# A value bias moved from the values of x to the copy of the message in a graph attention kernel

## The reference

```
q_base = elu(q_encoding @ w_qin.T + b_qin)
for t in range(4):
    cmd = q_base @ w_qt[t].T + b_qt[t]
    xc = x_ctx * mask
    x_joint = [x_loc, xc, pl(x_loc) * pc(xc)]
    q = lin(x_joint, w_q, b_q)
    k = lin(x_joint, w_k, b_k) * lin(cmd, w_pk, b_pk)
    v = lin(x_joint, w_v, b_v) * lin(cmd, w_pv, b_pv)
    e = edge scores of q and k by edge type, leaky relu, absent edges at -9e15
    prob = softmax(e)
    message = prob @ v
    x_ctx = lin([xc, message], w_mu, b_mu)
y = lin([x_loc, x_ctx], w_cb, b_cb)
```

## Time and profile before

| | us |
|---|---|
| median of 3 runs | 588.87 |
| lowest and highest | 586.61, 593.03 |
| span of the profiled execution | 569.6 |
| median less span | 19.3 |
| TensorE busy in the span | 513.9 (90%) |
| VectorE busy | 431.6 (76%) |
| ScalarE busy | 399.8 (70%) |
| GpSimd busy | 286.4 (50%) |

### The profile page before, as it was taken

How to read it: one execution, slowest core, us unless ns; L and a number is a source line. 1 busy time by engine, 2 the same in 40 slices (tenths; PEclk the granted TensorE clock), 3 DMA queues, 4 the chain that set the end, 5 groups by cost and what they waited for, 6 DMA issues and landing times. The chain is left out here.

```text
span 569.6 us, 14419 instructions
## 1 busy us (share of the span) xinstructions
PE 513.9 (90%) x4673; PEld 342.2 (60%) x4673; DVE 431.6 (76%) x1156; ACT 399.8 (70%) x1150; POOL 286.4 (50%) x511
## 2 busy tenths in 40 slices
PE   5997699999999999999889999898999788789991
PEld 3665466666666666665345565555655445568880
DVE  3589878888888888886545577868777878897882
ACT  4557578888888888887557687666777656558991
POOL 0587742222222222110144365858687757377884
PEclk9998999999999999999989999999999989869996
DMA  8600999999999300000100000011114003425530
GB/s 346 279 2 7 280 264 271 255 268 256 270 261 267 95 0 0 1 2 0 38 0 2 2 2 2 30 31 39 38 49 169 29 30 96 123 95 137 136 86 11
DMA packets 48535, 60.77 MB, mean 107 GB/s; under 512 B 2488, under 2 KB 45509, under 8 KB 47574
## 3 DMA queue, kind: packets, MB, share of 16 engines
q1 hardware_dynamic: 45686, 53.59, 35.4%
q0 software_dynamic: 2784, 6.37, 3.2%
HBM read 18.30 MB, written 42.10 MB: 106 GB/s over the span
## 5 line engine op out<-in xcount | busy, mean ns | idle before, releaser
L1565 DVE TENSOR_REDUCE nm<-SC 128x8 f32<-128x1024 f32 x64 | 75.3, 1219 | 33.6 <-PE SC L1076 33.0
L1465 DVE TENSOR_REDUCE room_w<-SC 128x512 f32<-128x2048 f32 x32 | 73.3, 2290 | 13.8 <-PE SC L927 13.8
L2079 ACT ACTIVATE room_p<-ST 128x512 f32<-128x512 f32 (+1 forms) x96 | 64.1, 740 | 25.6 <-PE ST L1094 25.6
L600 POOL TENSOR_TENSOR spread<-parts,units 128x48 bf16<-128x48 bf16 x32 | 8.8, 275 | 119.8 <-DVE parts L1455 119.8
L1985 ACT ACTIVATE room_w<-room_w,shift 128x128 f32<-128x128 f32 x128 | 49.7, 390 | 20.4 <-DVE shift L1472 20.4
L1976 ACT ACTIVATE room_w<-ST,cv 128x128 f32<-128x128 f32 x128 | 36.5, 367 | 17.0 <-PE ST L942 17.0
L1113 PE MATMUL SC<-room_p,room_w 128*32 128x128 f32 x1024 | 35.3, 279 | 9.2 <-DVE nm L1565 7.7
L798 POOL DMA_INDIRECT out<-room_v,id_r x39 | 38.7, 993 | 9.4 <-issue 7.0
L942 PEld LDWEIGHTS ST<-room_w 128*128 128x128 f32 x256 | 33.0, 191 | 15.2 <-issue 13.0
L1994 ACT ACTIVATE room_w<-room_w,inv 128x128 f32<-128x128 f32 x128 | 41.0, 409 | 0.8 <-DVE inv L1477 0.8
L636 POOL TENSOR_TENSOR ctx_t<-room_w 128x512 f32<-128x512 f32 x24 | 30.5, 1270 | 21.9 <-PE SC L927 20.6
(11 more groups left out here) (297 smaller groups left out, 1398.4 us busy)
## 6 DMA issues: line engine op xcount, KB each, us to landing
sorted_rows<-w SPq DMA_DIRECT2D x8, 4290.0 KB, 43.7
room_v<-sorted_rows SPq DMA_DIRECT2D x39, 130.0 KB, 2.1
x_t<-xT SPq DMA_DIRECT2D x2, 1024.0 KB, 8.1
ctx_t<-adj SPq DMA_DIRECT2D x1, 2048.0 KB, 16.5
room_w<-x SPq DMA_DIRECT2D x8, 256.0 KB, 2.9
room_w<-mask SPq DMA_DIRECT2D x1, 1536.0 KB
w<-weights SPq DMA_DIRECT2D x1, 1228.0 KB, 8.6
x_t<-w SPq DMA_DIRECT2D x1, 1032.0 KB, 5.0
```

What stands on the lines that cost most here:

```text
L1465: dve.tensor_reduce(logit[:, :, :], SC[:, :, :].rearrange("p b (i m) -> p b m i", i=TYPES), AX_X, ALU.max)\
L1565: dve.tensor_reduce(nm[:, v % 2, 2 * PER_R * pair:2 * PER_R * (pair + 1)], SC[:, 2 * pair:2 * pair + 2, :].rearrange("p r (i n) -> p (r i) ...
L2079: act.activation(ex[:, v % 2, first:last, :], ST[:, first:last, :], ACT.Exp)\
```

## The change

GpSimd no longer adds b_v to `vx`, and VectorE no longer waits for it. Instead b_v is one of the bias columns. GpSimd makes once `cvb` = `cv` * b_v (a column for each round and batch). `message_out` adds it: the Copy with a scale column becomes Identity with a scale column and a bias column. b_v leaves the row vectors, and the wait for them moves behind the rounds.

```diff
@@ setup, GpSimd
+            pool.wait_ge(cmd_ready, CV_OUT)
+            pool.tensor_scalar(cvb[:, :, :].rearrange("p t b -> p (t b)"), cv[:, :, :].rearrange("p t b -> p (t b)"),
+                               bias("bv"), None, ALU.mult).then_inc(S("cvb_ready"), 1)
             pool.wait_ge(S("u_out"), 1)
@@ GpSimd
-            def add_bias(g):
-
-                pool.wait_ge(vx_even, g + 1)
-                pool.wait_ge(vx_odd, g + 1)
-                bs = slice(g * GB, (g + 1) * GB)
-                pool.tensor_tensor(vx[:, bs, :], vx[:, bs, :], R("bv").unsqueeze(1).broadcast_to([128, GB, D]), ALU.add)\
-                    .then_inc(S("vx_ready"), 1)
...
             pool.wait_ge(S("first_ready"), 1)
             first_products(0)
-            pool.wait_ge(in_bv, 16)
-            add_bias(0)
             first_context(1)
...
             first_locals(1)
-            add_bias(1)
...
-                if opens(s) and opens(s + 5):
-                    add_bias(s + 5)
...
+            pool.wait_ge(in_bv, 16)
             pool.wait_ge(S("va_zero"), 2)
@@ VectorE
             columns(0, 0, 0)
-            dve.wait_ge(S("vx_ready"), 1)
             v_out(0, 0)
...
-                    if opens(s + 4):
-                        dve.wait_ge(S("vx_ready"), s + 5)
                     v_out(s + 4, n)
@@ ScalarE
             def message_out(s, t, g):
                 act.wait_ge(msg_done, s + 1)
+                if isinstance(s, int) and s == 0:
+                    act.wait_ge(S("cvb_ready"), 1)
                 for b in range(GB):
                     scale = cv[:, bass.ds(t, 1), g * GB + b:g * GB + b + 1].rearrange("p t b -> p (t b)")
-                    op = act.activation(msg_s[:, b * N:(b + 1) * N], M[:, b, :], ACT.Copy, scale=scale)
+                    shift_v = cvb[:, bass.ds(t, 1), g * GB + b:g * GB + b + 1].rearrange("p t b -> p (t b)")
+                    op = act.activation(msg_s[:, b * N:(b + 1) * N], M[:, b, :], ACT.Identity, scale=scale, bias=shift_v)
                 op.then_inc(msg_evac, 1)
```

More of the change, by code:

```diff
@@ L45 @@
 BIAS = {n: i for i, n in enumerate(("qin", "pl", "pc", "q", "k", "mu", "cb", "pk", "pv", "qt0", "qt1", "qt2",
-                                    "qt3", "init", "iq", "ik", "ln1g", "ln1b", "bo"))}
+                                    "qt3", "init", "iq", "ik", "ln1g", "ln1b", "bo", "bv"))}
 NW_FIRST = WCOLS["wk"][0]
 RCOLS = {"iv": (0, 128), "bo": (128, 256), "bog": (256, 268), "ln1g": (268, 396), "ln1b": (396, 524),
-         "ln2g": (524, 652), "ln2b": (652, 780), "gate": (780, 792), "bv": (792, 920)}
-NR = 920
+         "ln2g": (524, 652), "ln2b": (652, 780), "gate": (780, 792)}
+NR = 792
 HEADS = 16
@@ L196, in build @@
         cv = sb("cv", [128, T_ITER, B])
+        cvb = sb("cvb", [128, T_ITER, B])
         bq_w1 = sb("bq_w1", [128, TYPES])
@@ L617, in _ @@
             place(1)
-            add_bias(2)
             pool.wait_ge(v_done, 2)
@@ L622, in _ @@
             place(2)
-            add_bias(3)
             bias_parts()
@@ L628, in _ @@
             first_products(4)
-            add_bias(4)
             pool.memset(pad_row, 0.0).then_inc(S("spread_ready"), 1)
@@ L1494, in _ @@
             columns(1, 0, 1)
-            dve.wait_ge(S("vx_ready"), 2)
             v_out(1, 1)
@@ L1500, in _ @@
             columns(2, 0, 2)
-            dve.wait_ge(S("vx_ready"), 3)
             v_out(2, 2)
@@ L1506, in _ @@
             columns(3, 0, 3)
-            dve.wait_ge(S("vx_ready"), 4)
             v_out(3, 3)
@@ L2222, in layouts @@
                  ("iq", f["in_proj_b"][:D]), ("ik", f["in_proj_b"][D:2 * D]), ("bo", f["out_proj_b"]), ("ln1g", f["ln1_g"]),
-                 ("ln1b", f["ln1_b"])):
+                 ("ln1b", f["ln1_b"]), ("bv", c["b_v"])):
         cols[:, BIAS[n]] = v
@@ L2234, in layouts @@
     rowvecs = np.concatenate([f["in_proj_b"][2 * D:], f["out_proj_b"], np.zeros(LOGITS, np.float32), f["ln1_g"], f["ln1_b"], f["ln2_g"],
-                              f["ln2_b"], f["b_group"], f["b_expert"].reshape(-1), c["b_v"]]).reshape(1, NR)
+                              f["ln2_b"], f["b_group"], f["b_expert"].reshape(-1)]).reshape(1, NR)
     return {"xT": np.ascontiguousarray(a["x"].transpose(2, 0, 1).reshape(128, TOK)),
```

## The result

| | before | after |
|---|---|---|
| median, us | 588.76 (8 runs) | 595.17 (8 runs) |
| lowest and highest | 586.61, 593.03 | 594.03, 598.29 |
| span of the profiled execution | 569.6 | 596.5 |

The ratio is 1.0122, with a 95% interval of 1.0095 to 1.0149, which is 5.6 to 8.8 us. The medians lie 6.4 us apart; the ratios given in this document come from the runs and are not the quotients of the medians (here 1.0109). The prediction was 595.1, +6.2.

The account below looks back on a forecast made before the run. TensorE, busy 90% of the span, bounds the kernel, so its waits in the steady rounds count in full. Steady part +6.6, end of rounds +0.7, opening -1.15 make +6.2 on 588.9: 595.1 us, range 589.5 to 600.5.

Parts of the forecast that it names:

- second operand, a step: ScalarE's message copy: the bias column adds 0.36 us a step, taken from L2105 against L1994, bounds 0 and 0.50.
- register operation, a loop step: Ahead of ScalarE's message copy: another address operation may come, 0.05 us in each of 16 loop steps, between 0 and 0.10.
- reaction to the parts' copy: TensorE's value product follows the end of ScalarE's parts' copy by 0.06 us; 0 to 0.14 considered.
- to spare, loop / written out: Between parts' copy and value product: ScalarE has 0.09 us to spare in 15 steps, 0.17 in 9.
- steady part: Rounds' steps from 84 to 252 us: delay reaches the value product less the spare time, +6.6 us, 5.1 to 8.5.
- end of the rounds: Two of the last updates already wait for the message copy; each gets 0.36 whole, +0.7 us.
- opening: First 84 us: without GpSimd's eight additions contention with VectorE falls, -1.15 us, range -2 to +1.
- the collision: Opening, behind the second cast's gain: GpSimd's L570 now falls on VectorE's L1469, costing 0.7 us more.
- the 0.3 lost at the end: Opening, following two steps: a cast or reduction meets GpSimd's L570 again, 0 to 1.1 us, taken as 0.3.
- Absorbed: Value product's wait for parts' copy has over 0.36 us to spare, so not slower: 588.4 us; chance 0.13.
- The opening with both spells of low clock gone: Opening returns 4.5 us as both low-clock spells, 1.7 us each, vanish: 591.7 us; chance 0.11.
- The operand free: Message copy: the second operand costs nothing from PSUM, 587.4 us; chance 0.05.
- The clock falling in the steady part: TensorE's clock falls now that it waits each step, 1.7 us a spell; four give 602 us; chance 0.08.

Follow-up runs that it names:

- experiment 2: Kernel before with the message copied by Identity with scale and a zero bias column, GpSimd's additions kept: 598.34 us against 588.74, ratio 1.0153.
- experiment 8: Kernel before with four idle one-column ScalarE copies ahead of each copy of the turned parts: 594.48 us against 587.24, ratio 1.0125.
- experiment 7: Kernel before with one idle one-column ScalarE copy ahead of each copy of the turned parts: 589.58 us against 587.24, ratio 1.0048.
- experiment 3: Changed kernel with the message copied by Copy with one operand, b_v left out: 587.89 us against 588.74, ratio 0.9987.
- experiment 6: Kernel before with parts' copy right behind the message and the value product's context half ahead of the turn: 586.31 us against 587.24, ratio 1.0003.
- experiment 4: Changed kernel with parts' copy right behind the message and the whole value product ahead of the turn: 595.14 us against 588.74, ratio 1.0104.
- experiment 5: Changed kernel with parts' copy right behind the message and, outside round 0, the value product's context half ahead of the turn: 586.78 us against 587.24, ratio 1.0004.

## Why the prediction was right

It named the mechanism and the place, and the steady part's size within 0.5 us. That the sum comes within 0.2 of the measured 6.4 is partly luck: the steady part cost 0.5 more than forecast, the opening gave back 1.0 more, and the times show more than the traces. Term by term:

| term | predicted | measured |
|---|---|---|
| second operand, a step | 0.36 | 0.36 |
| register operation, a loop step | 0.05 | 0.02 |
| reaction to the parts' copy | 0.06 | 0.11 |
| to spare, loop / written out | 0.09 / 0.17 | 0.04 / 0.12 |
| steady part | +6.6 | +7.1 |
| end of the rounds | +0.7 | +0.36 twice |
| opening | -1.15 | -2.14 |
| sum | +6.2 | +6.4 in the times, +5.3 at the first reduce, +5.7 at the last update |

**The operand.** Taken from L2105, whose source is another memory, it fitted to 0.01. The bounds of 0 and 0.50 were needed for the range, and neither end came.

**The reaction.** This term was mis-sized, and ScalarE isn't named as releaser of L881 either. I took 0.06 from how fast the load of L935 follows L1994, and used it for L892 and L2002. All 24 steps of after and of experiments 2 and 8, and the loop steps of experiment 7, show 0.11 or 0.12. The better figure stood in what I had read: the upper bound 0.14 was the smallest distance among the 24. So the room in the loop was half of what I had taken, and a step lost 7.1 / 23 = 0.31 us on average, not 6.6 / 24 = 0.27.

**The register operation.** No second one came; the one that is there grew by 9 ns. In the loop the message copy starts 0.24 us after the penalties' load (193.23 to 193.47), before 0.21. The two errors act against each other. With 0.34 for the loop steps and 0.25 for the others, 15 x 0.34 + 8 x 0.25 = 7.1 over the 23 intervals, as measured.

**The opening.** This was the weakest part: -2.14 instead of -1.15, and only in part for the reasons given. The table follows how far VectorE is ahead of its own time in before, at the same instruction of both traces (us):

| where | before | after | lead | gained, predicted | measured |
|---|---|---|---|---|---|
| maximum over the types | 52.53 | 51.67 | 0.86 | 0.43 - 0.36 | 0.86 |
| penalty behind the collision | 56.16 | 56.33 | -0.17 | -0.7 | -1.03 |
| pair of penalties behind the second cast | 60.51 | 59.13 | 1.38 | 1.08 | 1.55 |
| maximum behind these penalties | 63.87 | 61.42 | 2.45 | 1.0 | 1.07 |
| first value product (TensorE) | 88.41 | 86.27 | 2.14 | -0.3 | -0.31 |

The casts did come back, 1.09 and 1.08, and so did the long penalty (two in 2.37 us instead of 3.44). Ahead of the second cast a wait of VectorE for TensorE of 0.39 went as well. The collision that I had put at 0.7 came with 1.08, at L1461. (The collisions of L1458 that follow, 1.38 us at 64.34 and 1.20 at 71.35, were there before as well, at 66.79 and 73.97.) The message's 0.36 did not arrive: TensorE's L947 is idle 0.57 instead of 0.20, but VectorE sets the pace there. Against experiment 3, which has all but the operand, after is only 0.09 late at the maximum behind the penalties (61.42 against 61.33), and 0.14 at 81.37. It is 0.39 late at the first value product only because the step ahead of that is already 0.25 longer. So the 0.3 lost at the end fits its prediction by luck: it is mostly that step, not another collision. Experiment 2's 1.7 is the operand's share and a longer stretch of low clock. The prediction called itself wrong if the opening moved by over 2 us, and by 0.14 it did.

**The whole time.** "Around the span lie 17 to 23 us" was wrong; it is 1.8. The first trace of before was a short execution, and its span was not to be set against the median of others. The difference of the two kernels came out all the same, since each term was taken from a stage that hardly varies between two traces of before. At the start of the attention after is 5.3 us behind and at the last update 5.7; the times say 6.4. In all versions the time against before is higher than the first reduce alone would have it, by 0.2 us (experiment 6) to 1.9 (experiment 4: 6.4 against 4.5). Behind the first reduce the code is the same but for the last message, yet up to the first transpose of the experts it takes 211.1 to 214.0 us in the ten traces, so a surplus of this size can't be placed. It is not explained.

**The rivals.** Absorbed: refuted by the steps, though experiment 5 shows that it takes only another order for it to come true. The opening with both spells of low clock gone: both are there, and its price was wrong as well, since the first one moves nothing when it comes or goes (experiment 7). The operand free: 89 ns. The clock falling in the steady part: 1.00, with waits in each step.

No run shows a version that is told from before: experiments 5 and 6 are level with it. Experiment 5 is 1.2% under the change as it was made (ratios to before of 1.0004 and 1.0122).

## What to carry to other kernels

The room between two engines is the distance in the trace less the shortest distance at which that same pair can follow, not less the reaction of another pair. Work behind a wait costs its length less that room, though its engine be idle 30% of the span, when the idle time lies ahead of the wait. If that makes something late, look for an order in which the late piece has other work beside it, and move the part of a product that fits the gap, not the whole.

## What was not expected of the hardware

- TensorE's weight load follows the end of ScalarE's copy of 640 columns by 0.11 to 0.12 us; behind the scaling of the probabilities it follows by 0.05 or 0.06 (196.12 to 196.18 in after), behind the message copy by 0.06. Why the pairs differ is open. It is this distance, and not the 0.06, that says how much room there is.
- A register operation for an address grew from 46 to 55 ns as the instruction behind it got a second operand from the same register. There was no second operation.
- GpSimd's one product of 128x128 by a column took 0.94 us in after and 0.86 in experiment 2; a copy of the same size took 0.29, and a product by a column of 128x512 0.76 at its shortest. What decides is open.
- When VectorE and GpSimd started 0.1 us apart, the first was not held up, but the one behind it was: L1458, started at 54.58, took 0.68, L574, started at 54.68, 1.71 instead of 1.27, and VectorE's next instruction, L1461 at 55.18, 1.23 instead of 0.15. In before L570 started at 34.30 and the cast at 34.34 took 1.27 instead of 0.18.
- The granted clock of the opening changes between kernels that hardly differ there. Over 40 to 64 us it is 0.93 in both traces of before, after and experiment 2, 0.95 in experiment 6, and 1.00 in experiments 3, 4, 5, 7 and 8; over 64 to 84 us it is 1.00 in experiments 4 and 8, 0.83 in 2, 0.97 in 6, and 0.91 in the others. Only the second stretch was seen to move what follows. What decides is open.
- The stage of the experts takes 66 to 85 us in traces of kernels that do the same there. What decides is open.
